# Two of eight head pairs take one root, of a product made by VectorE, in the second attention

## The reference, cut to what matters

```python
diff_sq = maximum(q_norm_sq + k_norm_sq - 2.0 * qk, 0.0)
denom = maximum((1.0 - q_norm_sq) * (1.0 - k_norm_sq), 1e-06)
cosh_arg = maximum(1.0 + 2.0 * diff_sq / denom, 1.0)
distance = where(cosh_arg > 1.0, arccosh(maximum(cosh_arg, 1.0 + 1e-12)), 0.0)
attn = softmax(-distance, axis=-1)
out = einsum('bhnm,bhmd->bhnd', attn, v)
```

## Time and profile before

| what | value |
|---|---|
| time, median of 3 runs | 3040.18 us (3038.32 to 3042.10) |
| profiled execution, its own time | 3041.84 us |
| its span | 3040.1 us |
| PE busy | 2598.1 us (85%) |
| DVE busy | 2307.1 us (76%) |
| ACT busy | 2223.2 us (73%) |
| POOL busy | 1637.9 us (54%) |
| A1 in the span: start of ScalarE's first and last root | 1596.4 and 2615.4 us |

### The profile page before, as it was taken

How to read it: one execution, slowest core, us unless ns; L and a number is a source line. 1 busy time by engine, 2 the same in 40 slices (tenths; PEclk the granted TensorE clock), 3 DMA queues, 4 the chain that set the end, 5 groups by cost and what they waited for, 6 DMA issues and landing times. The chain is left out here.

```text
span 3040.1 us, 42347 instructions
## 1 busy us (share of the span) xinstructions
PE 2598.1 (85%) x12208; PEld 1727.1 (57%) x12208; DVE 2307.1 (76%) x4329; ACT 2223.2 (73%) x2497; POOL 1637.9 (54%) x1288
## 2 busy tenths in 40 slices
PE   7999979999799996999975878778687777589998
PEld 6877756666587774878852323223232232268887
DVE  7677756777566777898977788787787877498887
ACT  5555536656455555777849999999999999777776
POOL 4667642122266763545536676776756667334444
PEclk9999979999899997999976667766666767689999
DMA  3111111111111112111100000000000000021111
GB/s 134 42 56 41 41 23 41 44 43 43 51 42 56 41 41 96 45 43 45 51 0 1 1 1 1 0 1 1 1 1 1 1 1 1 22 92 56 42 55 42
DMA packets 24917, 101.62 MB, mean 33 GB/s; under 512 B 5856, under 2 KB 7904, under 8 KB 15680
## 3 DMA queue, kind: packets, MB, share of 16 engines
q1 hardware_dynamic: 23360, 99.51, 9.5%
q10 hardware_dynamic: 1408, 0.34, 0.0%
HBM read 82.33 MB, written 2.62 MB: 28 GB/s over the span
## 5 line engine op out<-in xcount | busy, mean ns | idle before, releaser
L1911 POOL TENSOR_TENSOR A_Y<-A_Y,A_U 128x2048 f32<-128x2048 f32 x86 | 390.0, 4558 | 222.1 <-ACT A_U L1958 222.1
L1994 DVE TENSOR_SCALAR A_U<-ps 128x1024 f32<-128x1024 f32 x256 | 309.0, 1217 | 127.0 <-POOL A_Y L1911 58.1
L2000 DVE SCALAR_TENSOR_TENSOR A_U<-ps,A_U 128x1024 f32<-128x1024 f32 x256 | 310.8, 1214 | 57.3 <-PE ps L2144 57.3
L2144 PE MATMUL ps<-A_QT,A_KT 9*128 9x512 f32 x512 | 180.8, 702 | 193.6 <-DVE A_U L2000 162.0
L477 POOL TENSOR_TENSOR F0b_h<-F0b_h,dn 128x512 f32<-128x512 f32 x128 | 212.0, 1661 | 111.9 <-DVE F0b_h L409 111.8
L477 POOL TENSOR_TENSOR F0a_h<-F0a_h,dn 128x512 f32<-128x512 f32 x128 | 212.1, 1662 | 104.6 <-DVE F0a_h L409 104.5
L2144 PEld LDWEIGHTS ps<-A_QT,A_KT 9*128 9x128 f32 x512 | 65.7, 252 | 329.6 <-DVE A_U L2000 237.4
L1911 POOL TENSOR_TENSOR dn<-dn,A_U 128x2048 f32<-128x2048 f32 x42 | 190.3, 4551 | 112.8 <-ACT A_U L1958 112.8
L1958 ACT ACTIVATE A_U<-A_U 128x2048 f32<-128x2048 f32 (+1 forms) x96 | 236.5, 2464 | 0.0
L2116 PE MATMUL ps<-A_Y,A_VA 128*32 128x512 f32 x688 | 228.9, 799 | 5.8 <-DVE A_OT L1893 3.0
L1350 DVE CUSTOM_DVE_ANT_0 ps<-ps,A_mask 128x256 f32<-128x256 f32 (+1 forms) x512 | 184.8, 421 | 58.6 <-PE ps L1430 57.8
(11 more groups left out here) (417 smaller groups left out, 8134.7 us busy)
## 6 DMA issues: line engine op xcount, KB each, us to landing
dn<-weight_rows SPq DMA_DIRECT2D x32, 1024.0 KB, 4.6
F1a_cwb<-weight_rows SPq DMA_DIRECT2D x16, 1024.0 KB, 4.6
F1b_cwb<-weight_rows SPq DMA_DIRECT2D x16, 1024.0 KB, 4.6
A_KZ<-A_KT SPq DMA_DIRECT2D x132, 48.0 KB
A_QZ<-A_qs SPq DMA_DIRECT2D x96, 64.0 KB, 2.0
dn<-in_down SPq DMA_DIRECT2D x2, 2048.0 KB, 12.2
stage<-in_up SPq DMA_DIRECT2D x1, 2560.0 KB, 13.8
X<-in_x SPq DMA_DIRECT2D x4, 512.0 KB, 7.0
```

What stands on the lines that cost most here:

```text
L1911: eng.tensor_tensor(flat(y_slot(m, h)), flat(y_slot(m, h)), flat(Um[:, h % UR]), ALU.add).then_inc(s["t_ready"], 1)
L1994: eng.tensor_scalar(u_step(n), d_pair(n), 0.0, None, ALU.max).then_inc(s["dp_vector"], 1)
L2000: eng.scalar_tensor_tensor(out=u, in0=g_pair(), scalar=CLAMP, in1=u, op0=ALU.min, op1=ALU.mult).then_inc(s["u_ready"], 1)
L2144: last = eng.matmul(ps[:, 4 + b, :], KT[r:r + 9, pair, kt * P:(kt + 1) * P], QT[r:r + 9, pair, :], start=True, stop=True)
```

## The change

For pairs 1 and 5 (the second pair of sets 0 and 2), VectorE makes the product u(u+1) of each head after the pair's last step, straight into the Y slot. It first drains, waits for the slot (`pvh_done`) and then counts `v_ready`. ScalarE takes one root of it in place, head by head, instead of the two joined ones. GpSimd's add is the same instruction and now adds u itself. Ln gets scale 2 and bias 1, Exp scale -1. The other six pairs of a chunk are as before.

```diff
@@ attn1
+                ONE_ROOT = (1, 5)
...
+                def products_by(c, h):
+
+                    return c * (2 * len(ONE_ROOT)) + 2 * len([n for n in ONE_ROOT if n < h // 2]) + h % 2
@@ scalar
-                            for h0 in range(0, H, 4):
-                                for h in (h0, h0 + 1, h0 + 2):
-                                    joined = h == h0 + 2
...
-                                    if not first or h >= YR:
-                                        eng.wait_ge(s["pvh_done"], c * PAIRS + h // 2 - 1)
-                                    eng.wait_ge(s["u_ready"], c * STEPS + TPC * (h // 2 + 1))
-                                    eng.activation(y, u, ACT.Sqrt, bias=1.0)
-                                    eng.activation(u, u, ACT.Sqrt).then_inc(s["s_ready"], 2 if joined else 1)
...
+                            def one_root(h):
+                                y = flat(y_slot(m, h))
+                                eng.wait_ge(s["v_ready"], products_by(c, h) + 1)
+                                eng.activation(y, y, ACT.Sqrt).then_inc(s["s_ready"], 1)
...
+                            for g in range(SETS):
+                                for pair in (2 * g, 2 * g + 1):
+                                    if pair in ONE_ROOT:
+                                        one_root(2 * pair)
+                                        one_root(2 * pair + 1)
+                                    elif pair % 2 == 0:
+                                        two_roots(2 * pair, 1)
+                                        two_roots(2 * pair + 1, 1)
+                                    else:
+                                        two_roots(2 * pair, 2)
...
+                                    if pair in ONE_ROOT:
+                                        eng.activation(y, y, ACT.Ln, bias=1.0, scale=2.0)
+                                    else:
+                                        eng.activation(y, y, ACT.Ln)
                                     eng.drain()
-                                    eng.activation(y, y, ACT.Exp, scale=-2.0).then_inc(s["y_exp"], 2)
+                                    eng.activation(y, y, ACT.Exp,
+                                                   scale=-1.0 if pair in ONE_ROOT else -2.0).then_inc(s["y_exp"], 2)
@@ vector
+                            def product(h):
+                                u = flat(Um[:, h % UR])
+                                eng.drain()
+                                if not first or h >= YR:
+                                    eng.wait_ge(s["pvh_done"], c * PAIRS + h // 2 - 1)
+                                eng.scalar_tensor_tensor(out=flat(y_slot(m, h)), in0=u, scalar=1.0, in1=u, op0=ALU.add,
+                                                         op1=ALU.mult).then_inc(s["v_ready"], 1)
...
                                     scale(n0 + i)
+                                    pair = 2 * g + i // TPC
+                                    if i % TPC == TPC - 1 and pair in ONE_ROOT:
+                                        product(2 * pair)
+                                        product(2 * pair + 1)
                                     after(i)
```

More of the change, by code:

```diff
@@ L103, in macaron @@
                           "recip_ready", "xa_ready", "xv_ready", "turned", "d_done", "g_done", "dp_vector", "u_ready", "s_ready",
-                          "t_ready", "y_exp", "pvh_done"]
+                          "t_ready", "y_exp", "v_ready", "pvh_done"]
             sems[n] = {k: sem(f"{n}_{k}") for k in kinds}
@@ L1948, in main @@
                                     turned_scalar(eng, i, first_bank(i))
-                            for h0 in range(0, H, 4):
-                                for h in (h0, h0 + 1, h0 + 2):
-                                    joined = h == h0 + 2
-                                    y = y_two(m, h) if joined else flat(y_slot(m, h))
-                                    u = u_two(h) if joined else flat(Um[:, h % UR])
-                                    if not first or h >= YR:
-                                        eng.wait_ge(s["pvh_done"], c * PAIRS + h // 2 - 1)
-                                    eng.wait_ge(s["u_ready"], c * STEPS + TPC * (h // 2 + 1))
-                                    eng.activation(y, u, ACT.Sqrt, bias=1.0)
-                                    eng.activation(u, u, ACT.Sqrt).then_inc(s["s_ready"], 2 if joined else 1)
-                                eng.preload_act_table_set("natural_log_exp_and_others")
[L1960 to L1963, removed]
@@ new lines, in free_slot, with two_roots @@
+                            def free_slot(h):
+                                if not first or h >= YR:
+                                    eng.wait_ge(s["pvh_done"], c * PAIRS + h // 2 - 1)
+                            def two_roots(h, n):
+                                y = y_two(m, h) if n == 2 else flat(y_slot(m, h))
+                                u = u_two(h) if n == 2 else flat(Um[:, h % UR])
+                                free_slot(h)
+                                eng.wait_ge(s["u_ready"], c * STEPS + TPC * (h // 2 + 1))
+                                eng.activation(y, u, ACT.Sqrt, bias=1.0)
+                                eng.activation(u, u, ACT.Sqrt).then_inc(s["s_ready"], n)
@@ new lines, in one_root @@
+                            def one_root(h):
[12 more added lines that the diff above has]
+                                        two_roots(2 * pair, 2)
+                                eng.preload_act_table_set("natural_log_exp_and_others")
+                                for pair in (2 * g, 2 * g + 1):
+                                    y = y_two(m, 2 * pair)
+                                    eng.wait_ge(s["t_ready"], c * H + 2 * pair + 2 + UR)
+                                    if pair in ONE_ROOT:
+                                        eng.activation(y, y, ACT.Ln, bias=1.0, scale=2.0)
+                                    else:
+                                        eng.activation(y, y, ACT.Ln)
```

## The result

The changed kernel takes 3171.84 us (median of 4 runs, 3170.41 to 3176.79) against 3040.20: +131.6 us, ratio 1.0436, 95% interval 1.0418 to 1.0454. Forecast: 3168. The profiled execution has its own time of 3176.8 and a span of 3175.1, 135.0 above the span before.

A forecast was written before the change was run, and what follows sets the result against it. The prediction took VectorE to decide from set 0 to set 1, though ScalarE is busiest. 11.0 + 5.85 = 16.9 us a chunk, 10 + 7 x 16.9 = 128 us in all, gave 3168 us, range 3100 to 3200.

The forecast's parts named there:

- Who bounds: Second attention: ScalarE paces the stretch, but VectorE is on the path from set 0 to set 1; 4.75 us off it in set 3.
- The product's own price: VectorE's new 128x2048 product: 2.28 us with nobody in the way, worked out from its 1024-wide step and 2560-wide subtraction.
- The turns: VectorE's products and GpSimd's adds block each other: product after release 2.15 us, add after a product 4.4 us.
- some 30 at 6.6: Sign at GpSimd's adds: of the 128, some 30 would last 6.6 us.
- Rivals 1 and 2: 1: one hold for both products, 3118 us, chance 0.10; 2: no turns, 3070 us, chance 0.10.
- Set 0: After burst 0, steady chunk: VectorE resumes 11.0 us later, and the joined root of set 1 comes 11.0 later.
- this wait moves with VectorE and is no slack: VectorE's 2.29 us wait for TensorE's factor before set 1's last scale follows VectorE's own step, so it absorbs nothing.
- Set 2: After burst 2: VectorE resumes 10.6 us later, leaving 5.85 us at the joined root of set 3 and the next chunk.
- its slack of 4.75 us in front of pairs 6 and 7 is used up: Set 3: VectorE's waits for GpSimd, 3.97 + 0.78 us, take up part of the 10.6 us delay.
- had taken TensorE as unchanged: Whole kernel: TensorE at its mean granted clock 0.68, with a few tenths a burst either way left to the range.
- The sum: Whole kernel: 16.9 us a chunk for seven chunks plus 10 in chunk 0, 128 us in all.
- Rivals 3 and 4: 3: ScalarE sets the pace, faster, 3017 us, chance 0.03; 4: every product waits a whole add, 3210 us, chance 0.04.

The follow-up runs named there:

- experiment 2: Changed kernel with the products left out, ScalarE taking one root of u itself: 3032.29 us, -8.2 against the kernel before.
- experiment 5: Changed kernel with same-kind VectorE instructions writing u back, ScalarE's roots, Ln and Exp as before the change: 3196.38 us, +154.6 against the kernel before.
- experiments 9: Changed kernel with pair 1's products behind the taking of q, k, v and pair 5's behind the four copies: 3130.67 us, +88.9 against the kernel before.
- experiment 4: Changed kernel with GpSimd's first-pair adds in set 0 waiting until both products are made: 3153.12 us, +112.7 against the kernel before.
- experiment 1: Changed kernel with the product's second input in PSUM instead of SBUF (values not the product's): 3082.94 us, +42.5 against the kernel before.
- experiment 3: Changed kernel with a pair's two products made as one 128x4096 instruction: 3104.07 us, +63.6 against the kernel before.
- pair 1 alone: Changed kernel with only pair 1 (set 0) taking one root: 3116.94 us, +75.1 against the kernel before.
- pair 5 alone: Changed kernel with only pair 5 (set 2) taking one root: 3097.56 us, +55.8 against the kernel before.
- 7, pair 5, PSUM: Changed kernel with only pair 5 taking one root and the product's second input in PSUM: 3048.64 us, +6.8 against the kernel before.
- 8, the same behind the copies: Only pair 5, second input in PSUM, products moved behind the four copies that open set 3: 3044.23 us, +2.4 against the kernel before.
- 8, the real product there: Changed kernel with only pair 5, its real SBUF product moved behind the four copies: 3071.90 us, +30.1 against the kernel before.

## Why the prediction was right, point by point

- **Who bounds: right.** VectorE paces set 0 to set 1. Without VectorE's part the gain is 8.2 us (experiment 2), and with it alone the loss sits at ScalarE's joined roots (experiment 5). It holds for the products' place in this change; where they or the adds come later (experiments 9 and 4), ScalarE is last.
- **The product's own price: right.** 2.28 us worked out from the earlier trace rows, 2.288 measured (experiment 1).
- **The turns: right, and the larger part.** Fifteen of the 16 second products take 6.42 to 6.46 us as against 6.5 forecast; that of chunk 0, with no add queued, takes 2.29. First ones take 2.7 to 5.1, mostly 4.2 to 4.9, by how much of an add is left. Thirty adds take 6.54 to 6.59 where "some 30 at 6.6" was forecast. Experiment 1 takes 89 of the 132 us away, experiment 3 half of it by halving the turns. The Trainium skill (SBUF — State Buffer, section "Who interferes with whom") has its rule for any VectorE instruction with two SBUF inputs and names `tensor_tensor` as one case, so it covers the product too. By that rule, the trace agrees: the scalar_tensor_tensor with one tensor as both inputs stands still behind an add, and not with its second input in PSUM (2.29 us). Rivals 1 and 2 fall with this: a second product held together with the first would have lasted 2.28 us, not a whole add and its own time, and neither was short beside a running add.
- **Set 0: forecast 11.0 us a steady chunk, measured 10.1** with pair 1 alone ((75.1 - 4.2) / 7; in chunk 0 VectorE resumes 5.46 us after its last scale, where it was 1.31 before: 4.2, forecast 4.6). In the changed kernel's own trace burst 0's last scale to burst 1's takes 9.4 us more a steady chunk. In the chunk shown the first add had run 2.8 us when burst 0 ended (2038.94 to 2041.77), not 2.2, so less of it was left to wait for. Some more comes back in burst 1, whose last scale waits 0.61 us for TensorE here (2083.45) where it waited 2.29: the prediction had said that this wait moves with VectorE and is no slack.
- **Set 2: forecast 5.85 us, measured 7.0** with pair 5 alone (55.8 / 8), and more where it was forecast: pair 7's first relu comes 8.1 us later there and 8.4 in the changed kernel. The failed step is "its slack of 4.75 us in front of pairs 6 and 7 is used up". The slack was not wholly VectorE's to spend. TensorE's fourth turn, its outputs and the factor of burst 3's first step stand behind the first copy, and VectorE waits 3.53 us for that factor (2134.88 in the changed kernel). TensorE and its clock in that place (timeline, and windows view with the columns of the earlier trace rows), the last two rows from the kernel before:

```profile
2127.25 1.11 PE L1822 MATMUL ps<-ident,up_lo 128*128 128x128 f32 x4 [10.59 <-DVE A_QT L1830]
2128.29 6.12 PE L2154 MATMUL ps<-A_Y,A_VA 128*32 128x512 f32 x16
...
2123.00:2127.20 4.20, 0.00 (x0) 0.00 (x0) 4.20 (x3) 0.57 (x1) 4.20 (x2) 0.50 0.00 0
2127.20:2134.30 7.10, 7.05 (x20) 1.93 (x20) 4.14 (x5) 7.00 (x4) 7.10 (x2) 0.57 0.00 0
...
2190.67 3.63 PE L2116 MATMUL ps<-dn,A_VA 128*32 128x512 f32 x16
2190.60:2194.30 3.70, 3.70 (x20) 0.92 (x18) 1.22 (x3) 3.70 (x2) 3.70 (x2) 1.00 0.00 0
```

  TensorE stood still for 10.59 us, and its granted clock was 0.50, the lower of its levels (1.2 GHz), when it began again. The 16 outputs took 6.12 us instead of 3.63 at a granted clock of 1.00. These 2.5 us are, as an estimate, the larger part of the wait of 3.53. The forecast had taken TensorE as unchanged.
- **The sum: 128 forecast, 131.6 measured, and this closeness is luck.** By the single pairs the error is -7 in set 0 and +9 in set 2. In the changed kernel's own trace burst 0's last scale to burst 1's costs 70 us in all as against 82, and burst 2's last scale to burst 3's 64 as against 46: -12 and +18. The mechanism is right, the two terms are not as good as the sum.
- **Rivals 3 and 4: fell.** ScalarE's waits at the joined roots are 3.65 and 5.94 us, not under one; the first products wait for the rest of an add, not for a whole one.
- **What experiments 4 and 3 left over.** The 9 us a chunk behind set 0 in experiment 4, where 5.4 to 7 were due, are the 67.7 + 3.3 us of set 2 in the table below. Of the 12 us that experiment 3 was better than worked out, the clock has a part; the rest lies between burst 0 and burst 1, which cost 41 us in all where some 50 were due, and is **open**. So is what decides which clock a chunk gets behind set 2.

## What to carry to other kernels

The engine with the highest busy share was not the one to relieve: 53 us came off ScalarE and 8 of them could be had. Look at who waits for whom at the last handover of each stage, and by how little; half a microsecond there, in the wrong direction, makes all the difference. Before work with two SBUF inputs goes to VectorE, look what GpSimd does at that moment: beside long adds each such instruction costs the rest of an add, its own time, and the add's delay, so few and wide ones are better than many, and a place in VectorE's order where no add runs is better still. A gap of one engine is free only if nothing that another engine needs stands behind it. And a difference of a few microseconds a chunk is to be read at equal granted clock, stretch by stretch, before it is put down to the change.

## What the runs showed of the hardware that was not expected

The chunks of the changed kernel do not have one length. From take of q to take of q they last 144.65 us (1907.46 to 2052.11) and 148.63 (2052.11 to 2200.74), and the others too are near 145 or 148. Of these 4 us some 3 lie in the second half of burst 3, the steps of pair 7. The windows view of this half in the chunk before 2052 and in the one after:

```profile
1997.00:2010.00 13.00, 11.93 (x52) 4.86 (x50) 11.91 (x13) 11.40 (x6) 5.09 (x2) 0.74 0.00 1
2142.00:2158.00 16.00, 15.55 (x52) 5.85 (x52) 11.89 (x14) 10.95 (x6) 8.55 (x2) 0.52 0.00 1
```

TensorE's granted clock is 0.74 in the short one, a mean over both levels of 2.4 and 1.2 GHz, and 0.52 in the long one, nearly all at the lower. TensorE is busy 11.93 of 13 us and 15.55 of 16. In the long one VectorE waits 0.46, 1.93 and 1.72 us for TensorE there (2149.20, 2153.58, 2157.66), in the short one 0.46 and 0.60 (2003.55, 2008.99).

The kernel before has both lengths as well. In every trace, before and after, these steps (pair 7's first relu to the last scale's end) last 13.3 to 13.5 us at a clock of 0.74 to 0.76 or, mostly, 16.1 to 16.7 at 0.54 to 0.57; chunk 0 and a few others lie between. The table gives, for the eight chunks together and as read from the timelines, how much longer than in the kernel before two stretches are, and how many chunks have the short form:

| kernel | last scale of burst 2 to pair 7's first relu | from there to burst 3's last scale | short ones of 8 |
|---|---|---|---|
| before | 0 | 0 | 1 |
| changed | +67.2 us | -2.8 us | 2 |
| experiment 1, second input in PSUM | +16.6 | -5.1 | 3 |
| 2, no product | -6.1 | -1.1 | 0 |
| 3, one product a pair | +28.4 | -11.8 | 5 |
| 4, adds behind the products | +67.7 | +3.3 | 0 |
| 5, VectorE's part alone | +77.7 | -2.7 | 2 |
| 6, pair 1 alone | -1.3 | -1.6 | 1 |
| 6, pair 5 alone | +64.7 | -14.2 | 6 |
| 7, pair 5, PSUM | +16.2 | -5.3 | 3 |
| 8, the same behind the copies | +1.2 | +3.4 | 0 |
| 8, the real product there | +26.8 | -2.7 | 2 |
| 9, both moved | +26.7 | +2.9 | 0 |

Each short form is worth some 3 us in this stretch, of which 0.5 to 1.7 is lost again by the end of the next burst 0. Which kernel gets how many of them I had not forecast. The second column is the change's own part. There set 2's forecast was 46 us, and 67 came; experiments 3 (26 forecast) and 8 with the real product (29) came out at 28.4 and 26.8. What decides between the two forms the rows do not tell.

The operation L1862 of the kernel before (L1867 after) lasts 0.17 us at 2087.58, where it lasted 2.23 beside an add; in experiment 4 it lasts up to 4.34. Burst 1 now ends when GpSimd is through. A delay moved the operation out of the way, for nothing gained: the next wait for an add is 5.34 us (2101.06) where it was 3.16.
